# Attention with a mixture of experts beside it: values matmuls and expert turns two score units later in TensorE's order

## What is computed

```python
xn = _layernorm(x, axis=-1)
x = x + _L0_attn_ref(xn, ...) + _L0_ffn_ref(xn, ...)
...
att = jnp.einsum('bhqd,bhkd->bhqk', q, k) * scale
att = jnp.where(causal, att, -jnp.inf)
att = jax.nn.softmax(att, axis=-1)
y = jnp.einsum('bhqk,bhkd->bhqd', att, v)
...
probs = jax.nn.softmax(jnp.einsum('bsd,ed->bse', x, choice_w), axis=-1)
G, I = jax.lax.top_k(jnp.swapaxes(probs, -1, -2), k)
x_in = jnp.take_along_axis(x[:, None, :, :], I[..., None], axis=2)
h = jax.nn.silu(jnp.einsum('bekd,edf->bekf', x_in, w1))
x_mlp = jnp.einsum('bekf,efd->bekd', h, w2)
out = jnp.zeros_like(x).at[b_idx, I].add(G[..., None] * x_mlp)
```

## Time and profile before

| | |
|---|---|
| median of 3 runs | 389.32 us |
| the profiled execution | 392.95 us |
| its span, first to last instruction | 390.8 us |
| mean granted clock of TensorE | 0.935 of full |
| busy: TensorE, ScalarE, VectorE, GpSimd | 84%, 76%, 55%, 33% of the span |
| scores (L1149), 640 matmuls | 107.9 us |
| values (L1166), 1280 matmuls | 154.9 us |
| exponentials (L695), 320 | 264.4 us |

### The profile page before, as it was taken

One profiled execution on the slowest core, in us unless ns is written; L12 is line 12 of the kernel. 1 busy time (PEld: TensorE's weight loads), 2 busy tenths in 40 slices (PEclk: granted clock), 3 DMA queues, 4 the chain that ended last, 5 costly groups with the idle time before them and its releaser, 6 DMA issues.

```text
span 390.8 us, 7404 instructions
## 1 busy us (share of the span) xinstructions
PE 329.0 (84%) x2453; PEld 109.4 (28%) x2453; DVE 216.1 (55%) x605; ACT 296.0 (76%) x376; POOL 130.2 (33%) x123
## 2 busy tenths in 40 slices
PE   1775415789999879997999889999998899999981
PEld 0443401212222212221222223232332232323361
DVE  6859354776756786838656643252237442434553
ACT  1398134949999769995989898979888989898810
POOL 8321350740000000007770002857567414415160
PEclk9998555969999989999899999999999999999996
DMA  5053319540020110102430202324234403131157
GB/s 162 0 195 106 127 54 346 152 128 31 2 69 23 41 62 36 51 2 76 136 94 22 91 28 57 62 47 110 42 88 91 115 31 53 13 70 14 13 85 215
DMA packets 33679, 30.69 MB, mean 79 GB/s; under 512 B 3688, under 2 KB 28480, under 8 KB 33648
## 3 DMA queue, kind: packets, MB, share of 16 engines
q1 hardware_dynamic: 27248, 24.00, 19.1%
q0 software_dynamic: 6400, 6.30, 10.1%
HBM read 14.36 MB, written 15.93 MB: 77 GB/s over the span
## 4 chain that ended last, share of the span: by engine, by line
PE 64%; DVE 16%; ACT 6%; issue 6%; DMA 3%; POOL 2%; POOLq 0%; DVEq 0%; SPq 0%; ACTq 0%
PE bank L1166 30%; PE bank L1149 20%; PE bank L1227 4%; PE bank L1235 4%; ACT probs L695 4%; DVE probs L1001 3%; PE bank L1199 2%; DVE onehot L944 1%; DVE parts L781 1%; DVE cand L898 1%; DMA xn<-total_dram 1%; DVE xn L730 1%; PE bank L1174 1%; DMA total_dram<-m_space,token 1%; PE bank L1077 1%
## 5 line engine op out<-in xcount | busy, mean ns | idle before, releaser
L695 ACT ACTIVATE probs<-bank 128x1024 f32<-128x1024 f32 (+3 forms) x320 | 264.4, 929 | 45.4 <-PE bank L1149 42.3
L1166 PE MATMUL bank<-probs,v_grp 128*32 128x512 f32 (+3 forms) x1280 | 154.9, 557 | 9.6 <-DVE probs L1001 8.9
L1149 PE MATMUL bank<-q_aug,k_aug 51*128 51x512 bf16 (+3 forms) x640 | 107.9, 361 | 17.3 <-ACTq L677 12.8
L603 POOL DMA_INDIRECT total_dram<-m_space,token x32 | 50.6, 1580 | 97.5 <-DVE m_space L989 90.2
L1149 PEld LDWEIGHTS bank<-q_aug,k_aug 51*128 51x128 bf16 x640 | 27.8, 93 | 165.3 <-ACT probs L695 100.3
L1001 DVE TENSOR_TENSOR probs<-probs,causal 128x256 f32<-128x256 f32 x128 | 50.1, 422 | 40.1 <-ACT probs L695 30.1
L944 DVE TENSOR_SCALAR onehot<-slot_iota,slot 128x512 bf16<-128x512 f16 x128 | 36.9, 355 | 12.1 <-PE bank L1199 10.1
L1166 PEld LDWEIGHTS bank<-probs,v_grp 128*32 128x32 f32 x1280 | 25.5, 109 | 49.1 <-issue 19.2
L580 POOL DMA_DIRECT2D w_x<-in_L_ffn_w_dram x8 | 7.5, 943 | 94.4 <-DVE gate L963 94.4
L583 POOL DMA_INDIRECT parts<-xn_dram,token x32 | 32.0, 1001 | 9.7 <-issue 9.7
L977 DVE COPY m_space<-bank 128x512 f32<-128x512 f32 x16 | 11.0, 688 | 23.7 <-PE bank L1227 21.7
(11 more groups left out here) (128 smaller groups left out, 242.8 us busy)
## 6 DMA issues: line engine op xcount, KB each, us to landing
y_dram<-y_acc SPq DMA_DIRECT2D x16, 256.0 KB
q_aug<-product_dram SPq DMA_DIRECT2D x32, 96.0 KB
k_aug<-product_dram SPq DMA_DIRECT2D x32, 96.0 KB
w_x<-in_L_ffn_w_dram POOLq DMA_DIRECT2D x16, 128.0 KB
product_dram<-parts SPq DMA_DIRECT2D x4, 384.0 KB, 3.2
product_dram<-parts SPq DMA_DIRECT2D x6, 256.0 KB, 2.8
product_dram<-parts SPq DMA_DIRECT2D x2, 768.0 KB, 5.0
x_sb<-in_L_attn_x_dram SPq DMA_DIRECT2D x4, 256.0 KB, 3.6
```

The lines of the kernel that those rows point to most:

```text
L603: pool.indirect_dma_start(total_dram, bass.IndirectOffsetOnAxis(ap=token[:, e, t:t + 1], axis=0), y_exp[:, e % 2, t, :], None, compute_op= ...
L695: act.activation(probs[:, (u // 2) % PB, 2 * p:2 * p + 2, off:N], scores[u % SB][:, :, off:N], ACT.Exp, scale=SCALE).then_inc(s_exp, 1)
L1149: last = pe.matmul(scores[u % SB][:, a, off:N], k_aug[HEAD_ROWS[a], p, j * P:(j + 1) * P], q_aug[HEAD_ROWS[a], p, c * N + off:(c + 1) * N] ...
L1166: last = pe.matmul(acc[32 * h:32 * h + 32, off:N], v_grp[:, j, h, :], probs[:, k % PB, h, off:N], start=(k in CHUNK_START), stop=(k in CHU ...
```

## The change

`LEAD` goes from `SB` (3) to `SB + 2` (5). And in VectorE's group loop, the mask of the next step is written ahead of the copy of the sums in steps that end a chunk; in all other steps it stays where it was.

```diff
@@ -57,7 +57,7 @@
     NU = 2 * NS
     SB = 3
     PB = 4
-    LEAD = SB
+    LEAD = SB + 2
@@ -1010,6 +1010,8 @@
                 dve.tensor_copy(v_grp[:, :, :, 0:D], src).then_inc(s_vgrp, 1)
                 mask(g, 0)
                 for k, (c, j) in enumerate(STEPS):
+                    if k + 1 < NS and k in CHUNK_END:
+                        mask(g, k + 1)
                     if k in CHUNK_END:
 
                         dve.wait_ge(s_pfree, PB + NS * g + k + 1)
@@ -1017,7 +1019,7 @@
                         dve.tensor_copy(y_acc[:, c % 2, :], acc).then_inc(s_accfree, 1)
                     if k in turns and turn_first:
                         turn(turns.index(k))
-                    if k + 1 < NS:
+                    if k + 1 < NS and k not in CHUNK_END:
                         mask(g, k + 1)
                     if k in turns and not turn_first:
                         turn(turns.index(k))
```

## The result

The changed kernel takes **407.21 us** (median of 4 runs, 406.49 to 408.19), the kernel before 389.73 (4 runs). The ratio is 1.0447, with a 95% interval from 1.041 to 1.0483: slower by 17.5 us, where 17.4 were forecast. The profiled execution took 407.60 us, its span is 405.5.

What follows compares the result with a forecast made beforehand. TensorE, hardly ever waiting in the last two groups' attention loop, was taken as the bound. Terms 9.9 + 5.1 + 4.2 - 3.3 + 1.5 = 17.4 us took the median from 389.3 to 406.7 us; range 396 to 412.

Steps and rivals of the forecast that it cites:

- The tanh: In 8 experts, tanh waits for VectorE's copy at the head of ScalarE's queue, delaying exponentials and then scores: +9.9 us.
- Group ends: At 3 group ends, last values stand behind two scores waiting for new exponentials, delaying the next group's first values: +5.1 us.
- Other chunk ends: Next chunk's full scores run beside narrow values, so TensorE waits for exponentials; last two groups 3.0, search 1.2: +4.2 us.
- Waits that go: TensorE's waits for hT, before a transpose, for some masks and at the start shrink; narrow scores cost 0.7: -3.3 us.
- The clock: TensorE's clock falls once more, at one of the two group ends where there is no fall now: +1.5 us.
- a hidden tanh: Rival: the tanh's wait stays off TensorE because ScalarE has time to spare; 396.8 us, chance 0.12.
- The faster case: Rival: values no longer wait for fresh exponentials and masks, and neither tanh nor group end bites; 380.9 us, chance 0.05.
- No effect: Rival: three banks hold scores where they were and each step costs TensorE the same work; 389.3 us, chance 0.05.
- The rule of the Trainium skill: Rival: short idles between matmuls cycling through PSUM banks lower the clock in each expert; 12 us more, 418.7, chance 0.07.

Runs made afterwards that it cites:

- e1: The changed kernel with the tanh of turn k queued behind exponential 2k+6 in place of 2k+4 on ScalarE: 397.99 us, ratio 1.0189.
- e5: The kernel before (lead of three) with the tanh of turn k queued behind exponential 2k+2 in place of 2k+4: 400.94 us, ratio 1.0284.
- e2: The changed kernel with only three units of the next group ahead of a group's last values, fourth and fifth behind them: 401.48 us, ratio 1.031.
- e6: The kernel before with five units of the next group ahead of a group's last values, none in step 0 of groups 1 to 3: 400.11 us.
- e4: The kernel before with only the changed mask order at chunk ends, lead still three: 389.85 us, ratio 0.9987.

## Why the prediction was right

The median came out at 407.21 against 406.7, and the two chief terms were taken apart by runs. That the sum came within 0.5 us of the time is in part luck, since errors of its terms cancel. The terms one by one:

1. *The tanh, +9.9.* Right in place and mechanism. 9.4 us over the eight experts in the trace; taking it away gave 9.2 (e1), adding it alone cost 10.8 (e5). In the expert shown the waits came to 0.89 and 0.25 us, where 0.95 and 0.29 were computed; the full exponentials in a row start 0.90 apart there (five in 4.66), not 0.92.
2. *Group ends, +5.1.* Right in mechanism: 1.59 and 2.51 us for the two scores. The first values came at 5.1 to 5.4 us, 0.1 to 0.4 later than computed. At the ends with 5.3 and 5.4 the clock had already fallen ahead of them; the 5.08 of group 3 came at full clock in e1 too. Undoing it gave 5.7 with the clock's part in it (e2), adding it alone cost 10.0 (e6), where terms 2 and 5 make 6.6: together they were sized low. The prediction gave the whole cost to VectorE's chain behind the last values. e2 shows a second cause behind it, TensorE's own sixth and seventh score with the transposes between them, which held the first values at 4.2 us when the chain was short.
3. *Other chunk ends, +4.2.* In the last groups two waits of 0.19 and 0.24 us at a chunk's end (242.02 to 242.74 for two units that take 0.53, and 243.10 to 243.34): 0.43 x 6 = 2.6 where 3.0 were forecast. The row with 0.17 us stands in the trace at all six ends. In the search group there is 0.30 us at each of the two ends (at 90.51 and 111.25), where 0.6 was forecast, and 0.5 at the group's first chunk end (at 70.31 and 71.23), for which nothing was. This term was sized somewhat high.
4. *Waits that go, -3.3.* The 3.0 us before the second product and the transpose went. The 0.5 us of masks in the last groups did not: TensorE's waits for masks there were 0.8 us and are 1.1, now all at the groups' first values. At the start the first values wait 2.2 us in place of 3.5, since two more units stand in the wait; 0.5 was counted for that. The masks of the search group stayed, and for the reason given: the values come 2.46 us after the search matmul, in the last two rows here, as they came 2.41 after it in the earlier trace rows.

```profile
106.48 0.23 PE L1176 MATMUL bank<-above,ones_pp 128*128 128x128 bf16 x1
...
108.94 0.64 PE L1168 MATMUL bank<-probs,v_grp 128*32 128x256 f32 x8 [0.42 <-DVE probs L1001]
```

5. *The clock, +1.5.* It fell at both ends, not at one, which makes about 3. And it stayed low for longer at the start of group 1, where it had fallen before too and the term allowed nothing: 0.50 in the whole of 142 to 148 us, where the earlier trace rows has 0.72. In all six kernels with a lead or a group end of four or five units a window of 6 us at this start shows 0.50 to 0.52; of the four without, one does (e4). So this term was mis-sized low. Together with the terms that came out smaller (1, 3) that comes out about even. The near hit of the sum is better than the hits of its parts.

Of the rivals, a hidden tanh (396.8) is refuted by e1 and e5. The faster case asked for exponential 2k+7 at 4.2 us after the product; it came at 5.12 (291.50, computed 5.17), and the score behind it waited in the way computed. "No effect" holds for the second half of the change alone (e4). The rule of the Trainium skill ("TensorE: Matmul & The Clock Gate", "A second HAM failure mode: psum-queue depth-cycling") would have had the clock fall at the waits inside each expert. The trace doesn't show that: the values after them take 1.06 us, as ever. In the last two groups it fell at their starts alone, where TensorE is idle for more of the time: from the first unit to the first values of group 3 it is busy for 2.74 of 5.0 us.

## What to carry to other kernels

With three banks a lead of more than three units brings no score forward that has to wait for its bank; it moves everything else in that engine's order one place back, and every other engine's queue that was written against the old order has to be moved with it. Before changing such a lead, go through the other engines' queues and ask at each wait what stands behind it: here one tanh at the head of ScalarE's queue cost half of the loss. And where the profile shows short waits of the bound engine, look for their own cause first; both of the ones that the lead took away went by one argument in VectorE's order.

## What the runs showed that I had not expected

- The rows of a stretch do not by themselves tell whether the clock falls behind it. In the changed kernel TensorE is busy for 3.69 of the 6 us from 302.0, where group 3 starts, and the next 6 us have 0.80. In e1 it is busy for 3.70 of the 6 us from 297.5, at the same place with the same rows, and the next 6 us have 1.00. At the start of group 1 the prediction read 3.93 of 6 us busy and then 0.72; e4 shows 3.93 of 6 and then 0.51, and e5, with the same instructions there, this:

```profile
138.00:144.00 6.00, 3.93 (x38) 1.11 (x38) 4.68 (x16) 4.36 (x6) 0.00 (x0) 1.00 0.35 111
144.00:150.00 6.00, 4.69 (x50) 1.40 (x50) 5.45 (x19) 3.66 (x7) 0.00 (x0) 1.00 0.14 38
```

  So a fall counted from one trace is one draw, and what decides it stays open here.
- In one profiled execution of the kernel before ScalarE started an exponential some 2 us later than any row explains, which is part of why its group 1 took 2.4 us more than in e4. The cause stays open.
